# Mixture of experts behind gated cross-attention: narrow tiles' first products with the rows as weights, turned back by transposes, and four gather buffers

## The reference

```
x = x + tanh(g0) * attention(ctx, layernorm(x))       # 16 x 256 rows of 256, 8 heads of 128
z = layernorm(x)
gates = z @ Wg + bg;  two best of E = 8 experts, weights = softmax of the two
h_e  = silu(z @ W1[e] + b1[e])                         # 256 -> 1024
y_e  = h_e @ W2[e] + b2[e]                             # 1024 -> 256
out  = x + tanh(g1) * sum over the two of weight * y_e
```

## Time and profile before

| | us |
|---|---|
| median of 3 executions (1586.48 to 1591.55) | 1588.81 |
| profiled execution, its own time | 1595.61 |
| its span, first to last instruction | 1593.9 |
| PE busy | 1527.2 |
| DVE busy | 1110.4 |
| ACT busy | 952.3 |
| POOL busy | 635.0 |

### The profile page before, as it was taken

The page is one execution under the profiler, slowest core; times in us unless marked ns, Lnnn a source line. Parts: engine busy times, 40 slices in busy tenths (PEclk is TensorE's granted clock), DMA queues, the critical chain, the costliest instruction groups (busy, mean ns, idle before and its releaser), DMA issues. The chain is left out here.

```text
span 1593.9 us, 30347 instructions
## 1 busy us (share of the span) xinstructions
PE 1527.2 (96%) x10553; PEld 1411.5 (89%) x10553; DVE 1110.4 (70%) x2742; ACT 952.3 (60%) x2074; POOL 635.0 (40%) x782
## 2 busy tenths in 40 slices
PE   3999999999999999999999999998999999999897
PEld 3888898888988889888898888988899999999896
DVE  4667677777777777777777777777876666666452
ACT  4555556555565555655556555566777777777463
POOL 4423335334353443534435334243544544544221
PEclk9999999999999999999999999999999999999797
DMA  7000000000000000000000000035464554544441
GB/s 160 1 9 12 28 8 22 8 21 28 8 21 8 21 28 8 21 8 21 27 8 21 8 21 14 8 101 133 112 183 125 138 140 124 148 130 122 133 136 16
DMA packets 69441, 91.15 MB, mean 57 GB/s; under 512 B 21001, under 2 KB 56646, under 8 KB 69166
## 3 DMA queue, kind: packets, MB, share of 16 engines
q1 hardware_dynamic: 53470, 70.24, 14.3%
q0 software_dynamic: 15824, 18.98, 6.8%
HBM read 70.91 MB, written 18.29 MB: 56 GB/s over the span
## 5 line engine op out<-in xcount | busy, mean ns | idle before, releaser
L835 POOL TENSOR_SCALAR probs<-probs,rsum 128x512 f32<-128x512 f32 x256 | 174.0, 691 | 493.4 <-DVE rsum L1424 483.0
L1016 ACT ACTIVATE pt_hi<-turn 128x512 fp32r<-128x512 f32 x256 | 139.2, 596 | 241.4 <-PE turn L1141 241.4
L860 POOL DMA_INDIRECT out_rows<-yo,token x71 | 120.9, 1703 | 244.7 <-DMA out_rows<-yo,token 121.4
L174 PE MATMUL ph<-xt_hi,w1s_lo 128*128 128x256 f32 (+1 forms) x640 | 185.2, 289 | 9.6 <-DVE xt_lo L1519 9.2
L1536 DVE TENSOR_TENSOR ht_lo<-hs,ht_hi 128x512 fp32r<-128x512 f32 x142 | 98.2, 692 | 136.5 <-ACT ht_hi L995 135.1
L176 PE MATMUL ph<-xt_hi,w1s_hi 128*128 128x256 f32 (+1 forms) x640 | 182.8, 286 | 0.0
L175 PE MATMUL ph<-xt_lo,w1s_hi 128*128 128x256 f32 (+1 forms) x640 | 182.7, 286 | 0.0
L987 ACT ACTIVATE hs<-ph,b1t 128x256 f32<-128x256 f32 (+1 forms) x320 | 124.2, 447 | 97.7 <-PE ph L176 97.7
L1418 DVE TENSOR_REDUCE smax<-score 128x1 f32<-128x512 f32 x256 | 168.0, 682 | 11.6 <-PE score L176 11.4
L939 ACT ACTIVATE probs<-score,nbias 128x512 f32<-128x512 f32 x256 | 172.5, 683 | 3.8 <-DVE nbias L1420 3.8
L1611 DVE TENSOR_TENSOR pt_lo<-turn,pt_hi 128x512 fp32r<-128x512 f32 x256 | 164.0, 681 | 7.8 <-ACT pt_hi L1016 7.7
(11 more groups left out here) (220 smaller groups left out, 4679.1 us busy)
## 6 DMA issues: line engine op xcount, KB each, us to landing
w_raw<-in_L_ffn_W SPq DMA_DIRECT2D x45, 1024.0 KB, 18.5
xhat_rows<-rows SPq DMA_DIRECT2D x16, 264.0 KB, 2.2
x_raw<-in_x SPq DMA_DIRECT2D x16, 256.0 KB, 2.9
c_raw<-in_ctx SPq DMA_DIRECT2D x16, 256.0 KB, 3.1
out_rows<-x SPq DMA_DIRECT2D x16, 256.0 KB, 2.2
kv_raw<-in_L_xattn_Wkv SPq DMA_DIRECT2D x4, 512.0 KB, 6.5
xg<-xhat_rows,token POOLq DMA_INDIRECT x71
out_rows<-yo,token POOLq DMA_INDIRECT x71
```

The source lines that it names most:

```text
L174: pe.matmul(out, ll, rh, start=start, stop=False, **kw)
L835: last = pool.tensor_scalar(probs[n % 2][:, t, :], probs[n % 2][:, t, :], rsum[:, n % 2, t:t + 1], 1.0, ALU.mult, ALU.mult)
L860: pool.indirect_dma_start(out=A["out"], out_offset=bass.IndirectOffsetOnAxis(ap=token[:, u:u + 1].bitcast(U32), axis=0), in_=yo[t % N_YO][ ...
L1016: act.activation(pt[0][:, 2 * t:2 * t + 2, :], turn[t][:, :].rearrange("p (j i) -> p j i", j=2), ACT.Copy).then_inc(s_pthi, 1)
```

## The change

For narrow tiles the two operands of the first products change places: the tile's 128 rows are the weights, and W1 streams 256 columns. 12 products make a step, in place of 24. The result has the rows on the partitions ("flat"). DVE copies it from PSUM to SBUF (`read_flat`), PE turns it back with four fp32 transposes a step (`turn_hidden`) into the unused `routing` bank or `ph2`, and silu reads that. With this the order of the narrow steps is written anew: PE `turn_x`, `hidden(n)`, `turn_hidden(n-1)`, `out(n-2)`; ACT next rows (in the first step of a tile), silu and high part of n-1, W1 of n+2; DVE `read_flat(n)`, next rows (first step) or `finish(t-1)` (second step), low part of n-1, W1 of n+2. W1's two parts of a step are split by one instruction of 1024 elements on each engine. Narrow tiles gather into four buffers (the four halves of the two), three tiles ahead. Narrow tiles keep their split rows in halves of one `xt` buffer; `flat` lies over the other. Wide tiles keep their instructions.

```diff
-X_TURN = {step_of(t) + min(1, steps_of(t) - 2) for t in range(1, N_TILES - 1) if t + 1 != EARLY} | {step_of(EARLY) - 1}
-X_SPLIT = {step_of(t) + min(2, steps_of(t) - 1) for t in range(N_TILES - 1) if t + 1 != EARLY} | {step_of(EARLY) - 1}
+X_TURN = ({step_of(t) + (t < WIDE) for t in range(1, N_TILES - 1) if t + 1 != EARLY} | {step_of(EARLY) - 1})
+X_SPLIT = {step_of(t) + 2 for t in range(WIDE) if t + 1 != EARLY} | {step_of(EARLY) - 1}
...
+            with ExitStack() as narrow:
+                flat = [alloc(narrow, f"flat{i}", [P, KD * TILE]) for i in range(2)]
...
-                w1s=[[alloc(third, f"w1s{i}_{s}", [P, KD, PART_W], F32R) for s in pair] for i in range(N_W1S)],
+                w1s=[alloc(third, f"w1s_{s}", [P, N_W1S, KD, PART_W], F32R) for s in pair],
...
+        def xg_of(t, s):
+            n = t - WIDE
+            return xg[t % N_XG][s] if n < 0 else xg[t % N_XG][n // N_XG % SUB]
+
+        def s_gathered(t):
+            return s_g[t % N_XG] if t < WIDE else s_gn[(t - WIDE) % N_GN]
+
         def gathered(t):
 
-            return sum(subs(i) for i in range(t % N_XG, t + 1, N_XG))
+            return sum(subs(i) for i in range(t % N_XG, t + 1, N_XG)) if t < WIDE else (t - WIDE) // N_GN + 1
+
+        def had_rows(t):
+
+            n = t - WIDE
+            return t - N_XG if n < N_XG else WIDE - N_XG + n % N_XG if n < N_GN else t - N_GN
...
+        def xt_of(t):
+
+            if t < WIDE:
+                return [s[:, :, :] for s in xt[t % N_XT]]
+            c = (t - WIDE) % 2 * P
+            return [s[:, :, c:c + P] for s in xt[WIDE % N_XT]]
...
+        FIRST_N = step_of(WIDE)
+
+        def flat_of(n):
+            return ph[(FIRST_N + (n - FIRST_N) % 2) % N_PH]
+
+        def flat_sb(n):
+            return flat[(n - FIRST_N) % 2]
+
+        def turned_of(n):
+            return (routing, ph[(FIRST_N + 2) % N_PH])[(n - FIRST_N) % 2]
...
             def gather(t, s):
                 if t >= N_XG:
 
-                    pool.wait_ge(s_px, t - N_XG + 1)
-                    pool.wait_ge(s_w, row_of(t - N_XG + 1))
+                    pool.wait_ge(s_px, had_rows(t) + 1)
+                    pool.wait_ge(s_w, row_of(had_rows(t) + 1))
                 u = row_of(t) + s
                 source = dram["xhat"][0:EARLY_B * T, :] if t < EARLY else dram["xhat"]
                 pool.indirect_dma_start(
-                    out=xg[t % N_XG][s][:, :], out_offset=None, in_=source,
+                    out=xg_of(t, s)[:, :], out_offset=None, in_=source,
                     in_offset=bass.IndirectOffsetOnAxis(ap=token[:, u:u + 1].bitcast(U32), axis=0),
-                ).then_inc(s_g[t % N_XG], 16)
+                ).then_inc(s_gathered(t), 16)
...
-                if t + N_XG < N_TILES:
-                    for s in range(subs(t + N_XG)):
-                        gather(t + N_XG, s)
+                for later in (t + N_XG, t + N_XG + 1):
+                    if later < N_TILES and (later < WIDE + N_XG) == (later == t + N_XG):
+                        for s in range(subs(later)):
+                            gather(later, s)
...
+            def w1_hi_two(t, part):
+                buffer, filled = w1_at(t)
+                act.wait_ge(s_w1[buffer], 16 * filled)
+                act.wait_ge(s_ph, used_by(t - 1, part + 1))
+                act.activation(two_parts(w1s[0], part), raw_parts(t, part), ACT.Copy).then_inc(s_w1hi, 2)
...
             def silu(n, e):
                 t, j = TILE_OF[n]
-                act.wait_ge(s_ph, n + 1)
+                if t < WIDE:
+                    act.wait_ge(s_ph, n + 1)
+                else:
+                    act.wait_ge(s_th, n - FIRST_N + 1)
                 if n >= N_HS:
                     act.wait_ge(s_hlo, n - N_HS + 1)
                 for g in range(blocks_of(t)):
-                    last = act.activation(by_step(hs[n % N_HS], t)[:, g, :], by_step(ph[n % N_PH], t)[:, g, :], ACT.Silu,
+                    last = act.activation(by_step(hs[n % N_HS], t)[:, g, :],
+                                          by_step(ph[n % N_PH] if t < WIDE else turned_of(n), t)[:, g, :], ACT.Silu,
...
+            for n in range(FIRST_N, N_STEPS + 1):
+                if n < N_STEPS and TILE_OF[n][1] == 0 and TILE_OF[n][0] + 1 < N_TILES:
+                    hi_x(TILE_OF[n][0] + 1)
+                if n > FIRST_N:
+                    if TILE_OF[n - 1][1] == 0:
+                        e = expert_of(act, TILE_OF[n - 1][0])
+                    silu(n - 1, e)
+                    hi_h(n - 1)
+                for t, part in w1_parts(n + LEAD)[::2]:
+                    w1_hi_two(t, part)
...
+                if t >= WIDE:
+                    if n < FIRST_N + 2:
+                        pe.wait_ge(s_silu, n - N_PH + 1)
+                    else:
+                        pe.wait_ge(s_flat, n - FIRST_N - 1)
+                    for g in range(2):
+                        for k in range(KD):
+                            last = product(pe, flat_of(n)[:, g * PART_W:(g + 1) * PART_W],
+                                           [s[:, k, :] for s in xt_of(t)], [s[:, 2 * j + g, k, :] for s in w1s],
+                                           k == 0, k == KD - 1)
+                    last.then_inc(s_ph, 1)
+                    return
...
+            def turn_hidden(n):
+
+                pe.wait_ge(s_flat, n - FIRST_N + 1)
+                pe.wait_ge(s_silu, n - 1)
+                for g in range(2 * PB):
+                    last = pe.transpose(turned_of(n)[:, g * P:(g + 1) * P], flat_sb(n)[:, g * P:(g + 1) * P],
+                                        ident[:, :])
+                last.then_inc(s_th, 1)
...
+                if FIRST_N < n <= N_STEPS:
+                    turn_hidden(n - 1)
                 if n >= LAG:
                     out(n - LAG, at[TILE_OF[n - LAG][0]])
...
+            def read_flat(n):
+                dve.wait_ge(s_ph, n + 1)
+                if n >= FIRST_N + 2:
+                    dve.wait_ge(s_th, n - FIRST_N - 1)
+                dve.tensor_copy(flat_sb(n)[:, :], flat_of(n)[:, :]).then_inc(s_flat, 1)
...
-                if t and j == min(2, steps_of(t) - 1):
+                if t and j == 2:
...
+            for n in range(FIRST_N, N_STEPS + 1):
+                if n < N_STEPS:
+                    t, j = TILE_OF[n]
+                    read_flat(n)
+                    if j == 0 and t + 1 < N_TILES:
+                        lo_x(t + 1)
+                        take_weights(t + 1)
+                    if j == 1:
+                        finish(t - 1)
+                if n > FIRST_N:
+                    lo_h(n - 1)
+                for t, part in w1_parts(n + LEAD)[::2]:
+                    w1_lo_two(t, part)
```

More of the change, by code:

```diff
@@ L36 @@
 WIDE = (ROWS - NARROW) // 2
-assert 2 * WIDE + NARROW == ROWS
+assert 2 * WIDE + NARROW == ROWS and WIDE % 2
 SUB = 2
@@ L424, in layer @@
              "most", "most_at", "home", "order_f", "order_i", "is_place", "begin"))
-        (w2, hs, names, home_b2, expf, diag, ht, xt, yo, b2, w1_raw, xg, w1s, w2_raw) = (
-            work[n] for n in ("w2", "hs", "names", "home_b2", "expf", "diag", "ht", "xt", "yo", "b2",
+        (w2, hs, names, home_b2, expf, diag, ht, xt, flat, yo, b2, w1_raw, xg, w1s, w2_raw) = (
+            work[n] for n in ("w2", "hs", "names", "home_b2", "expf", "diag", "ht", "xt", "flat", "yo", "b2",
                               "w1_raw", "xg", "w1s", "w2_raw"))
@@ L494, in layer @@
         s_b1, s_b2, s_home_b2 = sem("b1_in"), sem("b2_in"), sem("home_b2_in")
+        N_GN = N_XG * SUB
         s_g = [sem(f"gathered{i}") for i in range(N_XG)]
+        s_gn = [sem(f"gathered_narrow{i}") for i in range(N_GN)]
+        s_flat, s_th = sem("flat_read"), sem("hidden_turned")
         s_diag, s_names, s_turned, s_token, s_tables = (
@@ L543, in used_by, with two_parts, raw_parts @@
             return step_of(t) + part * PB // blocks_of(t) + 1
-        def gathered(t):
-            return sum(subs(i) for i in range(t % N_XG, t + 1, N_XG))
+        def two_parts(tensor, part):
+            return tensor[:, part:part + 2].rearrange("p g k c -> p k g c")
+        def raw_parts(t, part):
+            return w1_raw[w1_at(t)[0]][:, :, part * PART_W:(part + 2) * PART_W]\
+                .rearrange("p k (g c) -> p k g c", g=2)
+        def xg_of(t, s):
[3 more added lines that the diff above has]
+            return s_g[t % N_XG] if t < WIDE else s_gn[(t - WIDE) % N_GN]
+        def gathered(t):
+            return sum(subs(i) for i in range(t % N_XG, t + 1, N_XG)) if t < WIDE else (t - WIDE) // N_GN + 1
[14 more added lines that the diff above has]
+            return (routing, ph[(FIRST_N + 2) % N_PH])[(n - FIRST_N) % 2]
         def by_step(function, t):
@@ L1046, in _ @@
             piece = W2_BEFORE
-            for n in range(1, N_STEPS):
+            for n in range(1, FIRST_N):
                 t, j = TILE_OF[n]
@@ L1158, in turn_x @@
             def turn_x(t):
```

(20 more changed lines are left out.)

16 lines of the change are left out of this document (8 added, 8 removed).

## The result

| | before | after |
|---|---|---|
| median | 1589.39 us (4 runs, 1586.48 to 1591.55) | 1563.4 us (4 runs, 1562.44 to 1564.86) |
| profiled execution, its own time | 1595.61 | 1564.09 |
| its span | 1593.9 | 1562.4 |

The ratio is 0.9838 with an interval of [0.982, 0.9857]: 26 us, where 32 were forecast; 1563.4 lies in the range.

What follows compares the result with a forecast made beforehand. Narrow-stage PE was held bound by product count, a 0.75 us pause per tile, a gather wait and half clock. The stage's 106.8 us became 70.2 (-36.6), plus 4.6 for gather waits: -32 from the median, 1557 us, range 1548 to 1575.

Steps and rivals of the forecast that it cites:

- the circle: Narrow tile's PE-DVE dependency loop through finish, register read, bias, weight, hidden split and PE's products: 7.35 us per tile.
- The wait before `xt_lo`: PE's pause at each narrow tile's start for the low half of the turned rows: 0.75 us, claimed to go.
- last tile, to the last scatter: End of the narrow stage: products, turns and waits for splits 12.8 us, then register read, bias, weight, issue 2.2.
- The 4.25 us of the first tile: First narrow tile, claimed shorter than 7.35 us because PE starts ahead of the helpers and the circle is not closed.
- Tile 32's 7.1: Second narrow tile, claimed at 7.1 us, shorter than 7.35 because the circle is not closed yet.
- Rival 3: Slower narrow tiles, by transposes at 0.2 us or scatter chains holding output buffers: 8.2 per tile, 1564 us; chance 0.08.
- The two waits: PE waiting for the gathers of tiles 34 and 35: 2.0 and 2.0 to 3.2 us, together taken as 4.6.
- Which I take not to come back: Narrow stage's 31 us at half clock, claimed not to return: 15.5 us saved.
- rival 1: Two gather waits let the clock fall again, costing 6.6 us, and waits grow by 4: 1568 us; chance 0.25.
- 36.6 - 4.6 forecast: Narrow stage: 36.6 us less if nothing else stops it, less 4.6 for gather waits; -32 in sum.
- Taking the whole difference from the median: Last step of the sum: the -32 us, built on the 1595.61 us profiled execution, subtracted from the 1588.81 median.
- the pace: Faster narrow tiles: nine times 2.1 us, less the longer end, 16 us saved.

Runs made afterwards that it cites:

- the repeated run: The kernel before, unedited, run and profiled again: 1587.2 us, ratio 0.9998 [0.9972, 1.0025].
- little of W1: Changed kernel with SP loading an eighth of W1's columns from tile 30 on, so those tiles compute with other weights: 1558.3 us, ratio 0.9812 against the kernel before.
- the two further edits: Changed kernel with finish(t-1) behind lo_h(n-1) on DVE and narrow gathers issued ahead of the wide scatter on POOL: 1559.8 us, ratio 0.9801 against the kernel before.
- gather first: Changed kernel with a narrow tile's gather issued before the wide tile's second scatter in POOL's loop: 1567.9 us, ratio 0.9844 against the kernel before.
- the best versions: Changed kernel with finish behind the low part and gathers ahead of scatters, with two or four output halves: 1559.8 and 1560.0 us, ratios 0.9801 and 0.9796 against before.

## Why the prediction was right, and where its sum was off

**The mechanism** held point by point. First products 115 ns (forecast 118), four transposes 0.36 us (0.45 with the switch), copy from PSUM 0.69 (0.69), tile 7.28 (7.35), the circle with its register reads as it was written, the wait of the next-to-last second products 0.52 and of the last 1.90 (0.55 and 2.0). The wait before `xt_lo` is gone.

**The stage** took 80.3 us in the profiled execution, forecast 74.8. Tile by tile, from the rows above:

| step of the forecast | forecast | measured |
|---|---|---|
| tile 31 | 4.25 | 6.3 |
| tile 32 | 7.1 | 8.1 |
| tile 33, without the wait | 7.35 | 7.56 |
| waits for gathers | 2.0 + 2.6 | 0 + 4.27 |
| tile 34 | 7.35 | 8.91 |
| tiles 35 to 37 | 22.05 | 21.84 |
| tile 38 | 7.1 | 7.3 |
| last tile, to the last scatter | 15.0 | 16.2 |

- *The 4.25 us of the first tile* is the step that failed most. In its two steps PE makes two sets of first products, one set of turns and, what the term left out, both sets of second products of the last wide tile: 2 x 1.47 + 0.45 + 2 x 1.48 = 6.35.
- *Tile 32's 7.1* left out DVE's wait of 1.93 us in `finish(30)` for its output buffer (L1668, released by the landing of a scatter of tile 28), behind which the split for PE's next second products is queued: PE stood 1.10. The forecast had named what is queued behind that instruction, but only with a wait on PE. Rival 3 had it, priced with the steady tile.
- *The two waits* were one. The gather of tile 34 went out at 1483.51 and was wanted only at 1488.60, as tile 31 and 32 were longer. That of tile 35 was later than forecast, as a scatter took 7.92 us to land. The sum was right within 0.3 us, by two errors of opposite sign.
- *"Which I take not to come back"* was wrong in part. Behind the wait of 4.27 us 15 products ran at 213 ns each and six transposes at twice their time, and so did the last 15 products of the stage: 1.6 and 1.4 us. The first of these is rival 1 at a quarter of its price. It held for the pauses of 0.3 us in the steady tiles, none of which brought the clock down.

**The time.** The stage's difference between the two profiled executions is 26.5 us (36.6 - 4.6 forecast), and yet their own times lie 31.5 apart, close to the -32 forecast: 5.5 us of it come from ahead of the first narrow product (1479.84 against 1474.33), where the change does nothing. Taking the whole difference from the median was itself a step that failed: the profiled execution of before was 6.8 us above its median, and the repeated run shows why. Its stage had 31 us at half clock and a longer gather wait, while the repeated run's stage took 99.6 us with some 14 at half clock (mean clock 0.93). So 15.5 us for the clock was too much for the median; from the repeated run it would have been 7. By the medians of the mean clock, before stood 35 to 45 us at half clock and after 20 to 22; at 0.44 to 0.57 us each that is 6 to 14 us of the 26.

**What the change is worth by its parts** is not as the forecast had it either. It gave 16 us to the pace (products and the missing wait together), 5 to the gather and 15.5 to the clock. The runs show that the two cheap parts, four gather buffers and the earlier split of the next rows, bring 21 us without any product changed. By the fitted price 8 to 11 of these are the clock (16 us at half clock, where before on the same chip had 35), and the rest the pauses themselves. The operand swap brings 5 to 6 more in its own order of work, 9 with little of W1, and some 11 with the two further edits.

What stays open: why scatters landed late in some tiles and not in others of the same run (4 to 8 us), beyond the part that W1's loads have in it, why gather first alone did not move the time, and how the 4 us of the best versions divide between their parts.

## What to carry to other kernels

A short pause of the tensor engine, repeated in every tile, is to be priced with the clock that it may cost: undo the pauses first, and all of them, since removing one of two brought a quarter or a half of what both brought. Before products are made faster, look at what the stage would follow next; here it was a circle through `finish`, and behind that a chain of scatters, each waiting for the landing of the one before. Profile the unedited kernel twice before a sum of waits is read as the work of an edit: POOL's wait for landings was 20.2 and 37.0 us in two executions of one kernel. And build the sum on a typical execution: where the profiled one is several microseconds above the median, find in which stage it lost them before a stage's saving is taken from the median.

## What the runs showed of the hardware that was not expected

- With products of 128 columns and a pause of 0.75 us every 9.4 us, the granted clock fell for some 3.4 us in three tiles, every second one, 20.5 us apart, and not in the next of that series; the same products without the pause held 1.00 for 66 us; in the profile of before the same pauses stood in a stretch of 58 us at 1.00. Before's spread of 17 us goes with its time at half clock; what decides when the clock falls is open.
- The same indirect scatter of 128 rows of 1 KB landed in anything from 3.6 to 7.9 us; with most of W1's loads away it took 3.7 to 4.8, and POOL never waited more than 3.2 us for one.
